# First layer's attention: a first pass four units ahead, the maxima turned inside the step, three late value groups, and the token copies on GpSimd

## The reference, cut to what matters

```python
def _L0_attn_ref(x, w_qkv, b_qkv, w_out, b_out, w1_rpe, b1_rpe, w2_rpe, b2_rpe):
    ...                                   # 16 heads of 8 features
    q, k, v = jnp.split(x @ w_qkv + b_qkv, 3, axis=-1)
    scores = jnp.einsum('bhtd,bhsd->bhts', q, k) / np.sqrt(D_HEAD)
    scores = scores + _rpe_bias(T, w1_rpe, b1_rpe, w2_rpe, b2_rpe)[None]
    attn = jax.nn.softmax(scores, axis=-1)
    out = jnp.einsum('bhts,bhsd->bhtd', attn, v)
    return out_transposed @ w_out + b_out
...
xn = _layernorm(x); s = _L0_attn_ref(xn, ...); g = _silu(_L0_ffn_ref(xn, ...)); x = x + s * g
xn = _layernorm(x); s = _L1_attn_ref(xn, ...); g = _silu(_L1_ffn_ref(xn, ...)); x = x + s * g
```

## Time and profile before

| | us |
|---|---|
| median of 3 runs | 1000.07 (997.71 to 1005.07) |
| the profiled execution | 1001.72 |
| its span, first to last instruction | 999.9 |
| TensorE busy in the span | 786.2 (79%) |
| VectorE busy | 645.5 (65%) |
| ScalarE busy | 509.3 (51%) |
| GpSimd busy | 411.4 (41%) |

### The profile page before, as it was taken

The page is one execution under the profiler, slowest core; times in us unless marked ns, Lnnn a source line. Parts: engine busy times, 40 slices in busy tenths (PEclk is TensorE's granted clock), DMA queues, the critical chain, the costliest instruction groups (busy, mean ns, idle before and its releaser), DMA issues.

```text
span 999.9 us, 19881 instructions
## 1 busy us (share of the span) xinstructions
PE 786.2 (79%) x6259; PEld 506.5 (51%) x6278; DVE 645.5 (65%) x1137; ACT 509.3 (51%) x883; POOL 411.4 (41%) x394
## 2 busy tenths in 40 slices
PE   0894787989988998854999999525598898989984
PEld 0652444555554554422555555314476666666663
DVE  6552786887788778832655655366356767676763
ACT  1243254676677766642433433258365555555542
POOL 7006776554555454421777777673210101010000
PEclk9996899999999999986999999856799999999997
DMA  5595745444544453142212222240665646464621
GB/s 141 194 192 138 174 121 123 97 94 102 123 115 92 100 122 88 31 136 59 58 53 53 58 55 54 78 122 16 142 135 124 148 117 159 115 157 117 136 58 51
DMA packets 132671, 106.13 MB, mean 106 GB/s; under 512 B 23317, under 2 KB 124633, under 8 KB 129545
## 3 DMA queue, kind: packets, MB, share of 16 engines
q1 hardware_dynamic: 122348, 91.23, 39.8%
q0 software_dynamic: 4352, 8.99, 2.9%
q10 hardware_dynamic: 5920, 5.24, 1.7%
HBM read 54.60 MB, written 50.03 MB: 105 GB/s over the span
## 4 chain that ended last, share of the span: by engine, by line
PE 27%; DMA 10%; DVE 7%; issue 4%; ACT 4%; SPq 2%; POOL 1%; DVEq 0%; ACTq 0%; POOLq 0%
PE ps L671 8%; DMA od_d<-ev 5%; PE ps L692 3%; PE ps L1567 3%; DVE mx L1272 3%; DMA rec<-od_d 2%; PE ps L683 2%; PE ps L665 2%; PE ps L1576 1%; ACT rows L893 1%; PE ps L673 1%; PE ps L1519 1%; SPq L1113 1%; PE ps L1517 1%; PE ps L1545 1%
## 5 line engine op out<-in xcount | busy, mean ns | idle before, releaser
L1272 DVE TENSOR_REDUCE mx<-ps 128x4 f32<-128x1024 f32 (+1 forms) x224 | 268.4, 1212 | 146.8 <-PE ps L1513 69.9
L1423 ACT ACTIVATE probs<-probs 128x1024 f32<-128x1024 f32 x128 | 131.8, 1051 | 64.9 <-DVE probs L1282 63.6
L1428 ACT ACTIVATE probs<-ps 128x1024 f32<-128x1024 f32 x96 | 96.8, 1024 | 82.9 <-PE ps L1545 55.8
L1202 POOL TENSOR_TENSOR qkr<-qkf,qk 128x512 f32<-128x512 f32 x27 | 31.3, 1160 | 244.0 <-ACT qk L1392 238.4
L1230 POOL TENSOR_TENSOR probs<-probs,tabB 128x1024 f32<-128x1024 f32 x42 | 99.5, 2369 | 74.6 <-ACT probs L1435 74.6
L1511 PE MATMUL ps<-tabA,eyeb 128*128 128x512 bf16 x256 | 102.3, 399 | 25.9 <-DMA ks<-parts_d 10.9
L1567 PE MATMUL ps<-probs,vpad 128*32 128x256 f32 (+1 forms) x2048 | 118.7, 362 | 4.2 <-ACT probs L1423 3.6
L1282 DVE TENSOR_TENSOR probs<-ps,tabB 128x1024 f32<-128x1024 f32 x86 | 101.5, 1210 | 4.3 <-PE ps L1539 4.3
L1513 PE MATMUL ps<-ks,qs 96*128 96x256 bf16 x512 | 102.3, 282 | 0.0
L1539 PE MATMUL ps<-qs,ks 99*128 99x256 bf16 x512 | 77.2, 280 | 6.8 <-DMA qs<-mT 2.6
L671 PE MATMUL ps<-qs,probs 128*128 x144 | 80.9, 644 | 1.4
(11 more groups left out here) (226 smaller groups left out, 1530.1 us busy)
## 6 DMA issues: line engine op xcount, KB each, us to landing
parts_d<-qk SPq DMA_DIRECT2D x64, 192.0 KB, 4.3
qs<-parts_d SPq DMA_DIRECT2D x32, 384.0 KB, 5.0
ks<-parts_d SPq DMA_DIRECT2D x32, 384.0 KB, 6.7
parts_d<-qk SPq DMA_DIRECT2D x64, 128.0 KB, 3.2
od_d<-ev SPq DMA_DIRECT2D x64, 128.0 KB
slots_in<-probs SPq DMA_DIRECT2D x1, 4680.0 KB
probs<-slots_in SPq DMA_DIRECT2D x72, 65.0 KB, 1.8
parts_d<-qk SPq DMA_DIRECT2D x64, 64.0 KB, 1.9
```

What stands on the lines that cost most here:

```text
L1272: nc.vector.tensor_reduce(mx[:, s.buf(), t, heads[0]:heads[-1] + 1], ring[:, slot].rearrange("p (h n) -> p h n", n=w), AX.X, ALU.max).then ...
L1423: nc.scalar.activation(probs[:, j, :], probs[:, j, :], ACT.Exp).then_inc(exp_done, 1)
L1428: nc.scalar.activation(probs[:, j, :], ring[:, slot], ACT.Exp).then_inc(exp_done, 1)
```

## The change

In the first layer only: the ring's order takes four first-pass units ahead of the second pass instead of three. The transpose of the maxima moves from the step's end to position 14, ahead of the second pass's unit 6, and `max_rows` on ScalarE from the end to position 12, behind exponential 4. Six of the eight units' values become late (three groups of two, in the next step at positions 3, 6 and 8), where there were two groups late; the first group is taken at position 12. The units whose bias GpSimd adds become 0, 2, 3 instead of 0, 2, 4, and GpSimd splits the maxima ahead of its third addition instead of behind it. The exponentials have the order 1, 0, 2, 4, 5, 6, 3, 7. From the third step on GpSimd copies the tokens for V (`tokens`), as the first thing of its step; in the three steps before, ScalarE goes on doing it. `scale`, `invert` and `project` move to positions 9, 15 and 11, ScalarE's `parts_one`, `outputs`, `parts_two` and `values` to 4, 7, 5 and 5. On SyncE the three part writes come first, then the outputs, the sums, the maxima, and the inverses last. The constants of the second layer keep its order.

```diff
-    def __init__(self, count):
+    def __init__(self, count, lead):
         self.count = count
-        self.order = [("A", 0), ("A", 1), ("A", 2)]
-        for j in range(count - 3):
-            self.order += [("B", j), ("A", j + 3)]
-        self.order += [("B", j) for j in range(count - 3, count)]
+        self.order = [("A", j) for j in range(lead)]
+        for j in range(count - lead):
+            self.order += [("B", j), ("A", j + lead)]
+        self.order += [("B", j) for j in range(count - lead, count)]
...
-    U = Units(8 if layer == 0 else 6)
+    U = Units(8, 4) if layer == 0 else Units(6, 3)
...
-    LATE = 2 if layer else 4
-    SCALE = 2 if layer else 0
-    INVERT = 7 if layer else 10
-    VALUES = {9: (0, 1)} if layer else {13: (0, 1), 15: (2, 3)}
-    ASIDE = () if layer else (0, 2, 4)
-    ORDER = tuple(range(NU)) if layer else (1, 0, 3, 2, 5, 6, 4, 7)
-    PROJECT = 10 if layer else 8
+    LATE = {0: (2, 3, 4, 5)} if layer else {3: (2, 3), 6: (4, 5), 8: (6, 7)}
+    VALUES = {9: (0, 1)} if layer else {12: (0, 1)}
+    SCALE, INVERT, PROJECT = (2, 7, 10) if layer else (9, 15, 11)
+    QK, V, TURN = (1, 4, NU * 2) if layer else (1, 5, 14)
+    ASIDE = () if layer else (0, 2, 3)
+    ORDER = tuple(range(NU)) if layer else (1, 0, 2, 4, 5, 6, 3, 7)
+    A_PART, A_OUT, A_TWO, A_VAL, A_MAX = (2, 0, 4, 4, NU * 2) if layer else (4, 7, 5, 5, 12)
+    SEQ = ((("take", 0),), (("exp", 1),), (("take", 2), ("exp", 0)), (("take", 3), ("exp", 2)), (("exp", 4),),
+           (("exp", 5),), (("exp", 6), ("exp", 3)), (("exp", 7),))
...
             # SyncE, first layer
+                    if s.has(2):
+                        parts(s, 0)
+                        parts(s, 1)
+                        parts(s, 2)
+                    if s.has(-2):
+                        outputs_out(s)
+                        sums_in(s)
+                        outputs_in(s)
+                    if s.has():
+                        maxima(s)
+                    if s.has(-2):
+                        inverses_out(s)
+                        inverses_in(s)
...
             # GpSimd
+            def tokens(s):
+                if s.has(-1):
+                    pool.wait_ge(v_full, s.n(-1) + 1)
+                nc.gpsimd.tensor_copy(xb[:], xnT[:, bass.ds(s.n() * T, T)]).then_inc(xb_done, 1)
+
             def body(s):
+                if s.has() and layer == 0 and s.k >= HELP:
+                    tokens(s)
...
                     if n == 1 and s.has(2):
                         rest_two(pool, nc.gpsimd, s)
+                    if n == 2 and s.has():
+                        parts_gpsimd(pool, s)
                     if s.has(-1):
                         bias_aside(pool, s, n, j)
...
-                if layer == 0 and s.has() and s.k >= HELP:
-                    parts_gpsimd(pool, s)
...
             # VectorE, before the third step
-                        if pos == 1 and s.k < HELP:
+                        if pos == 4 and s.k < HELP:
                             rest_one(dve, nc.vector, s)
-                        if pos == 4 and s.k < HELP:
+                        if pos == 7 and s.k < HELP:
                             rest_two(dve, nc.vector, s)
...
             # ScalarE
-                if s.has():
+                if (layer or s.k < HELP) and s.has():
...
                     nc.scalar.activation(xb[:], xnT[:, bass.ds(s.n() * T, T)], ACT.Copy).then_inc(xb_done, 1)
...
             # TensorE
+                for pos, (kind, j) in enumerate(U.order):
                     if s.has(-2):
-                        for j in range(first, last):
-                            values(s, -2, j)
...
+                        for i in LATE.get(pos, ()):
+                            values(s, -2, i)
-                    if pos == 1 and s.has(2):
+                    if pos == QK and s.has(2):
                         projections(s)
-                    if pos == 4 and s.has():
+                    if pos == V and s.has():
                         misc_free(pe, s, "V")
...
+                    if pos == TURN and s.has():
+                        turn_maxima(s)
```

More of the change, by code:

```diff
@@ L1165, in body @@
                     stacks(s)
[L1166 to L1179, removed]
-                if s.has():
-                    maxima(s)
+                if layer == 0:
+                    if s.has(2):
[11 more added lines that the diff above has]
+                        inverses_in(s)
+                else:
+                    if s.has(2):
+                        parts(s, 0)
+                    if s.has(-2):
+                        outputs_out(s)
+                    if s.has(2):
+                        parts(s, 1)
+                    if s.has(-2):
+                        sums_in(s)
+                        outputs_in(s)
+                    if s.has(2):
+                        parts(s, 2)
+                    if s.has(-2):
+                        inverses_out(s)
+                        inverses_in(s)
+                    if s.has():
+                        maxima(s)
             if layer:
@@ L1453, in body @@
                 for pos, (kind, j) in enumerate(U.order):
-                    if pos == (0 if layer else 4) and s.has(-2):
+                    if pos == A_PART and s.has(2):
+                        parts_one(s)
+                    if pos == A_OUT and s.has(-2):
                         outputs(s)
                     if kind == "B" and U.exists(s.k, kind):
[L1457 to L1462, removed]
-                    if pos == 1 and s.has(2):
-                        parts_one(s)
-                    if pos == 4 and s.has(2):
+                        for what, i in (SEQ[j] if apart(s.k) else (("exp", j),)):
+                            if what == "take":
+                                take(s, i, U.slot(s.k, pos))
+                            else:
+                                exponential(s, i, U.slot(s.k, pos))
+                    if pos == A_TWO and s.has(2):
                         parts_two(s)
-                    if pos == 4 and s.has():
+                    if pos == A_VAL and s.has():
                         values(s)
+                    if pos == A_MAX and s.has():
+                        max_rows(s)
                 if layer and s.has(-3):
@@ L1474, in body @@
                     act.dma_start(v.wdn, v.down_w.rearrange("e (c i) h -> i e c h", c=2)).then_inc(v.w_load, 16)
-                if s.has():
+                if A_MAX >= len(U.order) and s.has():
                     max_rows(s)
@@ L1577, in projections, with turn_maxima @@
                 mm.then_inc(qk_full, 1)
+            def turn_maxima(s):
+                misc_free(pe, s, "M")
+                pe.wait_ge(max_parts, 4 * (s.n() + 1))
+                nc.tensor.transpose(misc[0:PARTS * 2 * H, 0:P // 2].bitcast(BF16),
+                                    m3[:].rearrange("p c h t -> p (c h t)"), eyeb[:]).then_inc(mt_full, 1)
             def body(s):
-                def late_values(first, last):
+                for pos, (kind, j) in enumerate(U.order):
                     if s.has(-2):
-                        for j in range(first, last):
-                            values(s, -2, j)
[L1585 to L1590, removed]
+                        for i in LATE.get(pos, ()):
+                            values(s, -2, i)
+                    if pos == QK and s.has(2):
                         projections(s)
-                    if pos == 4 and s.has():
+                    if pos == V and s.has():
                         misc_free(pe, s, "V")
@@ L1620, in body @@
                             values(s, -1, i)
[L1621 to L1625, removed]
+                if TURN >= len(U.order) and s.has():
+                    turn_maxima(s)
             if layer:
```

## The result

| | us | ratio to before, 95% interval |
|---|---|---|
| median after | 974.21 (973.51 to 975.81) | 0.9757 [0.973, 0.9784] |
| median before, same chip | 998.89 (995.75 to 1005.07) | |
| profiled execution after | 975.81, span 974.0 | |

It was said 977, 971 to 988. The spans differ by 25.9 us, and the timelines divide that into five stretches. A0 stands for first-pass unit 0 of a step; "last exponential" is the end of the first layer's last one.

The account below looks back on a forecast made before the run. A ring of waits, not traffic or the sum of TensorE's work, was taken to set the 20.00 us step. Third step -0.6, eleven steps 22.1 and tail 2.0 sum to 23.5 us won: 977 us from 1000.07, range 971 to 988.

Parts of the forecast that it names:

- The period: First layer's full step: falls from 20.00 to 18.0 us, ended by one maximum, `project` and two additions on VectorE.
- the ring through the exponentials: Full step before the change: 4.7 us of TensorE, 10.8 of VectorE, 4.5 of ScalarE in sequence.
- the walk up to A7: TensorE's new order from first-pass unit 0 to unit 7: unit 7 starts at 13.09 us if nothing stops TensorE.
- What is late next: Turn of the maxima in the full step: only 0.3 us behind the ring; TensorE awaiting it over 0.8 means wrong.
- The third step: First layer: V waits for GpSimd's token copy behind the scatter; fourth step starts 0.6 us later, bounds 1.2 lost, 0.5 won.
- The scatter doesn't move: Third step: GpSimd stays held by 64 scatter DMAs until 170.40, as before the change.
- The tail: Last step's start to the first layer's last exponential's end: from 37.4 to 35.4 us, 2.0 won, between 1 and 3.
- The sum: Whole kernel: third step -0.6, eleven steps 22.1 and tail 2.0 give 23.5 us won.
- The step near the end: Step already without projections, before the change: read as still 20.00 us, so neither traffic nor TensorE's work sets the period.
- the second rival: Full steps: another ring also holds the 20 us period, only the tail is won, 999 us; chance 0.07.
- Exponentials that hold the turn of the step: Rival, full steps: exponential 3 comes 1.5 us late for the values, steps take 19.0, kernel 988 us; chance 0.12.
- shut each other out: Rival, full steps: `scale` locked out by GpSimd's second bias, period 20.6, kernel 1005 us; chance 0.04.

Follow-up runs that it names:

- turn at the end: Changed kernel with maxima turn and copy back at the step's end: 1039.14 us; the same with 14 unused products filling TensorE's pause: 1018.85 us.
- The filled pause: Changed kernel with twelve extra unused matmuls where TensorE waits in the step of the last second pass: 977.57 us, one run.
- split last: Changed kernel with GpSimd splitting the maxima behind its third bias addition again: 1026.01 us, ratio 1.0261.
- three ahead: Changed kernel with three first-pass units ahead instead of four, dependent positions shifted by one: 1014.61 us, ratio 1.0147.

## Why the prediction was right

- **The period.** The two edges that were to carry it hold. The turn inside the step and the copy of the maxima behind one exponential free the step from the ring through the exponentials (3.6 us by the two runs with the turn at the end), and VectorE's last maximum, `project` and two additions end it, as the run with `project` moved shows. 17.92 against 18.0; the 0.1 lies in the walk up to A7, which took the projections at 0.96, and they take 0.86 (307.11 to the next unit at 307.97). The fourth unit ahead is worth 1.4 us at an equal clock (19.32 to 17.92). What the third late group, the order of the exponentials, the units given to GpSimd and SyncE's order add was not run.
- **What is late next.** The turn, with TensorE waiting 0.66 us, inside the 0.8 that I allowed. I had put it 0.1 to 0.3 behind the path; with `project` out of the way the period fell by the full 0.33, with the turn a position later. VectorE's pauses lie ahead of maxima 6 and 7 as said, 0.61 and 0.54, and two more of 0.52 and 0.32 that I had not seen.
- **The third step.** Its mechanism was right: V stands behind the scatter, for 7.64 us, and swallows what the steps before gain. The size was off. "The scatter doesn't move" failed: GpSimd is free 72.9 us after A0 of step 0 (165.66 less 92.78), before 75.5 (170.40 less 94.93); in the other versions it was 70.7 to 74.7, so part of the difference may be spread between executions. The slow clock cost more than the 2.0 I took: 14.58 from V to A0 (166.20 to 180.78) less 12.0 walked is 2.6, my upper bound. Together 1.5 won in place of 0.6 lost. Why the scatter landed sooner was not tested.
- **The tail.** The walk was right and the result wasn't: the term left out that TensorE pauses 2.68 us there and goes on at half clock, so 2.0 won became 0.2 lost. The filled pause gives the 35.4 back.
- **The sum.** 23.5 was said of the first layer and 24.1 measured (1.49 + 22.74 - 0.16); the other 1.8 of the span are setup and the stretch behind, neither the change's. That the sum came so close is in part luck: the third step came out 2.1 us better than said and the tail 2.2 us worse, and the two misses cancel.
- **The step near the end.** I read it as still 20.00 us, but that is the length at which I cut the window. The maxima of the last two full steps before the change are copied at 405.75 and 424.90, 19.15 us apart: without the projections the step was 0.8 us shorter. That fits the ring that I walked, since the projections are in it, and takes away what spoke for the second rival. No term of the sum uses it.
- **The rivals.** Exponentials that hold the turn of the step would have shown a wait of the values on one; the period of 17.92 leaves no room for their 1.5 us. The period didn't stay. `scale` ran at 11.26 of the step (317.48) while GpSimd paused (2.07 us up to 319.00), so the two never met, and no run here shows whether they would have shut each other out.

What I missed is not in the changed kernel's full steps but around it: I treated TensorE's clock as a matter of the third step. The runs that undo one part show that it is a good part of what the parts are worth, since a step that lets TensorE stand can pay for it twice, for the wait and for the slow matmuls behind it: in full steps here always behind 2.7 us or more, and in seven steps of ten behind about 2.0.

## What to carry to other kernels

When a step is bound by a ring of waits, walk the ring with durations from one step, find the engine whose queue stands across it, and move the one short instruction that others need (here a 0.25 us copy) ahead of the long ones. Put what VectorE must do anyway into its pauses rather than into the chain at the end. Price a new wait of TensorE with the slow matmuls behind it, and don't hang a short operation on an engine that is held by something else, as the third step's tokens were.

## What was not expected of the hardware

TensorE's granted clock can drop to the lower of its two levels behind pauses as short as 1.9 us in a step that is otherwise nearly full, and equal pauses don't always do it. In full steps, pauses of 2.7 to 2.8 us (split last) and of 3.3 us (turn at the end) were each followed by matmuls at about half rate (1.92 for 1.04, and 2.07 for 1.03). Pauses of 1.91 to 2.02 us (three ahead) were so in seven steps of ten (0.63 for 0.38) and left the clock at 1.00 in three. Pauses of 0.65 to 0.95 us, after the change and before it, left 1.00 throughout. Work that nobody needs, put into the pause, made a step 2.4 us shorter. GpSimd copies 128x256 fp32 in 0.40 us, as fast as ScalarE does (0.40 at 322.09 where it copies all tokens), and in little over half of the 0.743 of a two-input operation of that shape.
